# A decoder layer on one core: shared weights split in thirds behind each step's work, up products inside the last four steps, the first SiLUs together, one bank for the last gate's chain

## The chip, the core and the metric

The kernel runs on one core of a Trainium2 chip. The time is that of the device, in microseconds: the median over runs. Profiles are of one execution each.

## What is computed

The reference is one pre-norm decoder layer in float32 on x (8 x 112 x 512), that is 896 tokens:

```
x = x + attention(layernorm(x))          # 16 heads of 128, causal
x = x + cross_attention(layernorm(x), ctx)   # 32 heads of 16, ctx 8 x 375 x 512, q and k rms-normalised
x = x + moe(layernorm(x))
moe(x):
  probs = softmax(x @ gate_w.T); two best of 8 experts, weights normalised
  out = (silu(x @ shared_gate.T) * (x @ shared_up.T)) @ shared_down.T      # inner width 704
  out += sum over the two experts e of w_e * (silu(x @ gate_e.T) * (x @ up_e.T)) @ down_e.T   # inner width 352
```

## The kernel before

Every large product is made of three (`mm3`, L505 to L507): each operand is held as a high part, rounded by ScalarE (`hi`, L953), and a low part, the difference, subtracted by VectorE (L1334) or GpSimd (L1864). Five instruction streams are written out by hand, one function for each engine, and wait for one another on semaphores (`w.wait_ge`). Each engine works in program order, so the order of the calls sets everything.

After the first attention comes the cross attention in NK = 48 steps (batch, half of the heads, a third of the context; `keys`). A step of TensorE (`step` in `tensor`) is: scores of step n (`score_pe`, L702); one thing aside, by turns a transposition of the last unit's output (`out_pe`, L729), a transposition of a normalised batch (`norm_turn`, L593) or a piece of the gate's logits (`gate_pe`); the key and value rows of step n + 4 (`rows_pe`, 12 products of 512 columns from `wkv` and `ctx`), which the last four steps don't have; the transposition of keys (`rows_turn`, L669); values of step n (`value_pe`, L719), which wait for the exponentials of ScalarE (`ee`, L1115). VectorE scales keys (`rq`, `rr`, `kn`), copies them (`kT`) and normalises batches.

The shared expert has six slices of weights (c = 0 to 5, each 128 x 1536 with gate, up and down parts; tiles SE, S1, S2, S0, S1, S2, loaded by SP into `sf_e`, `sf0`, `sf1`). For the first 448 tokens a slice needs: `s_hi_act` and `s_low` (split), `up_pe(0, c, a)` with a = 0 the gate and a = 1 the up product (12 products of 448 columns each), `up_silu`, `up_mul`, `up_hi`, `up_low`, and `down_pe(c, tiles)`, four tiles of three products with 512 columns, added up in banks 2 to 5. I call these up(c,a), silu(c), low(c), down(c). ScalarE has one table for exponential and logarithm and another for silu; a change is an ACT_TABLE_LOAD.

Before, slices 0, 1 and 2 are split ahead of steps 3, 43 and 45, whole on ScalarE, then one third on VectorE and two on GpSimd at the same time. up(0,0), up(0,1), up(1,0), up(1,1) follow the values of steps 44 to 47. The last batch is then normalised, transposed and sent through the gate, and VectorE works out the routing: softmax, two best experts, counts (`t_cum`), a small product on TensorE ("R"), the place of each row (`slot`), the expert of each unit (`eid`). Slices 3, 4, 5 are split and multiplied among this. Normalised rows (`rows_normal`, L1727) go to memory by 16 indirect transfers of GpSimd (`scattered`, L1965), in two groups of eight; SP then loads the gathered units (`xg`, L2116).

The second half is a list of jobs (`job_pe`): the shared expert for the other 448 tokens in three jobs, whose weights are `E` and `F` (`part_hi`, `part_low`), then 21 units of the experts. Its first product is at 787.74 us in the profile, the first transposition of `xg` (L813) at 817.93.

The wait that SP has between the routing and the first gathered unit, and the loads ahead of it, in the kernel's words:

```
                else:
                    w.wait_ge(*scattered[1, NB - 1])
                e.dma_start(xg[j % 4][:, :], slots_d[unit_of[j] * BS:(unit_of[j] + 1) * BS, 2:]).then_inc(*xg_in[j % 4].did(j))

            part_load(0, 0)
            part_load(0, 3)
            sf_load(5)
```

## Time and profile before

| | |
|---|---|
| median of 3 runs | 990.66 us (990.51 to 990.93) |
| the profiled execution | 991.74 us, its span 989.90 us |
| TensorE busy (PE) | 936.6 us, 95% |
| VectorE (DVE) | 553.5 us, 56% |
| ScalarE (ACT) | 452.4 us, 46% |
| GpSimd (POOL) | 192.9 us, 19% |
| chain that ended last | PE 86%, DVE 8%, ACT 2%, all others 1% or less |

A row of the timeline gives start, duration, engine, line, operation, result <- inputs, sizes and count; in brackets the idle time before it and what ended it. Matmuls overlap by their filling and draining, so start to start is the time that one takes up. "PEclk" is the granted clock: 1.00 is 2.4 GHz, 0.50 is 1.2 GHz. `bank` is a bank of PSUM. An index that the names have in the code is left out in the trace.

### The profile page before, as it was taken

Reading aid. Unit: us, or ns where it says so; the run is one execution under the profiler, and the core shown is the slowest. Engines: PE = TensorE matmul, PEld = TensorE weight load, DVE = VectorE, ACT = ScalarE, POOL = GpSimd, SP = SyncE. Lnnn points to the kernel's source line nnn. Section 1 sums busy time; section 2 is a strip of 40 time slices with the busy share of each in tenths; the row PEclk is TensorE's granted clock in tenths of the full one; section 3 lists DMA queues with packets and bytes.
Section 4 is the critical chain, followed back from the end, with each engine's and each line's share of the span. In section 5 each row is a group of like instructions: output and inputs, shape, how many; then the busy total and the mean of one; then the engine's idle time right before and its main releaser. Section 6 shows DMA issues by size and latency. Waiting matters only on the chain.

```text
span 989.9 us, 17898 instructions
## 1 busy us (share of the span) xinstructions
PE 936.6 (95%) x7250; PEld 811.3 (82%) x7250; DVE 553.5 (56%) x1178; ACT 452.4 (46%) x1100; POOL 192.9 (19%) x141
## 2 busy tenths in 40 slices
PE   4999999999999999989999999999788999999995
PEld 3999999999999999866777777777566788899994
DVE  6253535353535353765654654654527655888882
ACT  3342414141414152636665665665543233656651
POOL 1220202020202033302101101101111530222322
PEclk9999999999999999999999999999898999999998
DMA  5110632020202003141100100100112566899973
GB/s 185 66 44 21 223 101 66 22 73 17 76 17 71 2 22 128 43 128 55 33 12 22 33 12 23 32 13 2 65 33 101 202 208 234 276 308 290 294 208 42
DMA packets 31330, 94.12 MB, mean 95 GB/s; under 512 B 6177, under 2 KB 9489, under 8 KB 29329
## 3 DMA queue, kind: packets, MB, share of 16 engines
q1 hardware_dynamic: 26944, 83.80, 24.8%
q0 software_dynamic: 4304, 9.19, 4.7%
q8 instruction: 57, 0.93, 0.4%
q14 instruction: 25, 0.20, 0.1%
HBM read 74.33 MB, written 16.81 MB: 92 GB/s over the span
## 4 chain that ended last, share of the span: by engine, by line
PE 86%; DVE 8%; ACT 2%; issue 1%; DMA 1%; POOL 1%; SPq 0%; ACTq 0%; DVEq 0%
PE bank L505 23%; PE bank L506 22%; PE bank L507 22%; PE bank L702 4%; PE bank L719 4%; PE bank L577 3%; PE bank L552 3%; PE bank L669 2%; DVE E_lo L1334 1%; PE bank L564 1%; DVE rq L1473 1%; PE bank L813 1%; PE bank L729 1%; PE bank L593 1%; PE bank L821 1%
## 5 line engine op out<-in xcount | busy, mean ns | idle before, releaser
L1115 ACT ACTIVATE ee<-bank 125x448 f32<-125x448 f32 x192 | 91.1, 549 | 23.1 <-PE bank L702 22.1
L505 PE MATMUL bank<-xT_hi,wqk_hi 128*128 128x448 f32 x256 | 95.9, 375 | 1.4 <-DVE xT_lo L1334 1.4
L506 PE MATMUL bank<-xT_hi,wqk_lo 128*128 128x448 f32 x256 | 93.6, 366 | 0.0
L507 PE MATMUL bank<-xT_lo,wqk_hi 128*128 128x448 f32 x256 | 93.6, 366 | 0.0
L505 PE MATMUL bank<-wkv_hi,ctx_hi 128*125 128x512 f32 x192 | 81.3, 423 | 8.9 <-DVE kn L1486 8.0
L1334 DVE TENSOR_TENSOR E_lo<-F,E_hi 128x940 fp32r<-128x940 f32 (+2 forms) x62 | 80.8, 1330 | 1.6 <-ACT E_hi L953 1.5
L506 PE MATMUL bank<-wkv_hi,ctx_lo 128*125 128x512 f32 x192 | 77.0, 401 | 0.0
L507 PE MATMUL bank<-wkv_lo,ctx_hi 128*125 128x512 f32 x192 | 76.6, 399 | 0.0
L1864 POOL TENSOR_TENSOR ctx_lo<-ctx_f,ctx_hi 128x500 fp32r<-128x500 f32 x24 | 30.1, 1255 | 216.1 <-ACT ctx_hi L953 216.1
L505 PE MATMUL bank<-wv_hi,xT_hi 128*112 128x256 f32 x256 | 72.2, 282 | 0.0
L506 PE MATMUL bank<-wv_hi,xT_lo 128*112 128x256 f32 x256 | 71.7, 280 | 0.0
L507 PE MATMUL bank<-wv_lo,xT_hi 128*112 128x256 f32 x256 | 71.7, 280 | 0.0
L953 ACT ACTIVATE E_hi<-F 128x940 fp32r<-128x940 f32 (+2 forms) x62 | 67.6, 1147 | 1.1 <-PE bank L507 0.4
L1416 DVE TENSOR_TENSOR xa<-xa,bank 128x512 f32<-128x512 f32 x56 | 38.3, 687 | 53.1 <-PE bank L507 53.1
L1979 POOL DMA_INDIRECT out<-yg,meta x21 | 39.9, 1901 | 141.1 <-DMA out<-yg,meta 70.1
L1864 POOL TENSOR_TENSOR wqk_lo<-wqk_f,wqk_hi 128x1024 fp32r<-128x1024 f32 x16 | 37.8, 2363 | 145.0 <-ACT wqk_hi L953 145.0
L1495 DVE COPY kT<-bank 128x250 f32<-128x250 f32 x48 | 20.1, 418 | 79.8 <-PE bank L669 79.8
L1095 ACT ACTIVATE sq<-bank 125x256 f32<-125x256 f32 (+1 forms) x64 | 24.5, 383 | 83.6 <-PE bank L507 83.6
L953 ACT ACTIVATE qk<-bank 128x448 f32<-128x448 f32 x32 | 17.4, 544 | 97.6 <-PE bank L507 97.6
L1012 ACT ACTIVATE pp<-sm,nm 112x112 f32<-112x112 f32 x128 | 48.1, 377 | 30.3 <-DVE nm L1388 30.3
L505 PE MATMUL bank<-E_hi,xgT_hi 128*128 128x352 f32 x168 | 56.4, 336 | 0.6 <-DVE E_lo L1334 0.6
L507 PE MATMUL bank<-E_lo,xgT_hi 128*128 128x352 f32 x168 | 54.2, 323 | 0.0
(320 smaller groups left out, 2430.7 us busy)
## 6 DMA issues: line engine op xcount, KB each, us to landing
F<-wexp SPq DMA_DIRECT2D x14, 1408.0 KB, 7.5
F<-wexp SPq DMA_DIRECT2D x14, 768.0 KB, 7.3
wqk_f<-wqk SPq DMA_DIRECT2D x16, 512.0 KB, 3.3
ctx_f<-ctx SPq DMA_DIRECT2D x24, 250.0 KB, 2.7
slots<-zt SPq DMA_DIRECT2D x1, 5397.0 KB, 19.1
xg<-slots SPq DMA_DIRECT2D x21, 256.0 KB, 6.5
F<-moe SPq DMA_DIRECT2D x6, 768.0 KB, 6.1
wv_f<-wv SPq DMA_DIRECT2D x8, 512.0 KB, 3.4
```

Source lines behind the costliest of these rows:

```text
L505: e.matmul(out, a[0], b[0], start=first, stop=False)
L506: e.matmul(out, a[1], b[0], start=False, stop=False)
L507: return e.matmul(out, a[0], b[1], start=False, stop=last)
L702: i = e.matmul(SX[r][0:MS, g * 2 * T:(g + 1) * 2 * T], kT[n % 6][32 * r:32 * r + 32, g, :], qT[u % 2][32 * r:32 * r + 32, g, :, :], start= ...
L719: i = e.matmul(AB[32 * c:32 * c + VW, r * T:(r + 1) * T], vb[n % 6][:, 8 * (c // 2) + 2 * r + c % 2, :], ee[(4 * n + r) % 8][:, c * T:(c + ...
L953: return e.activation(out, src, ACT.Copy)
L1012: i = e.activation(pp[g][:, c, :], sm[g][:, c, :], ACT.Exp, bias=nm[g][:, c:c + 1], scale=ISQ, accum_out=rs[g][:, c:c + 1])
L1115: e.activation(ee[(4 * n + r) % 8][:, :], SX[r][0:MS, 0:4 * T], ACT.Exp, scale=0.25).then_inc(*x_exped.did((n, r)))
L1334: return e.tensor_tensor(out, src, high.bitcast(F32), ALU.subtract)
L1416: e.tensor_tensor(xa[:, j, :], xa[:, j, :], PJ[u][:, :], ALU.add).then_inc(*pj_dve.did(u))
L1864: return e.tensor_tensor(out, src, high.bitcast(F32), ALU.subtract)
L1979: e.indirect_dma_start(out_d, bass.IndirectOffsetOnAxis(ap=meta[:, unit_of[j], 0:1].bitcast(U32), axis=0), yg[j % 4][:, :], None, compute_ ...
```

## The change

- Slices are split in thirds of 512 columns (two for the gate and up parts, the last for the down part), on ScalarE and VectorE alone, behind the work of a step: slice 0 in steps 3, 4, 5, slice 1 in step 44, slice 2 in 45, slice 3 in 46. An up product waits for two thirds of its slice, a down product for the third.
- up(0,0) to up(1,1) come before the key transposition and the values of steps 44 to 47. The first gate and up results are copied out of their banks (`gate_keep`, `up_keep`), the silu is applied behind the last step; silu(0), silu(1), silu(2) follow one another there.
- The last gate's chain uses bank 3 alone, so that down products for banks 2, 5 and 4 can stand between; "R" moves behind up(3) to bank 7.
- VectorE's order in the routing is new; rows 0 to 3 are normalised before the expert numbers.
- The two groups of scatters wait for four transfers at a time.

Where lines with "..." stand, parts of the diff are left out.

```diff
-        TX, tx_before, tx_last = {}, {}, {7: ("p", 1), 3: ("s", 1), 4: ("s", 2)}
+        TX, tx_before, tx_last = {}, {}, {7: ("p", 1), 3: ("s", 1)}
         for n, u in enumerate(tx_uses):
-            i = 3 + (n - tx_turn) % 2 if n >= tx_turn else 7
+            i = 3 if n >= tx_turn else 7
             TX[u], tx_before[u], tx_last[i] = banks[i], tx_last[i], u
...
-        ups = [("u", 0, c, a) for c in range(3) for a in range(2)] + ["R"]
-        ups += [("u", 0, c, a) for c in range(3, NS) for a in range(2)]
+        ups = [("u", 0, c, a) for c in range(4) for a in range(2)] + ["R"]
+        ups += [("u", 0, c, a) for c in range(4, NS) for a in range(2)]
...
-        downs = [(0, 0, b) for b in (0, 3, 1, 2)] + [(0, c, b) for c in range(1, NS) for b in range(4)]
+        downs = [(0, c, b) for c, b in ((0, 0), (0, 3), (0, 2), (1, 0), (1, 3), (1, 2), (0, 1), (1, 1), (2, 0), (2, 3), (2, 2), (2, 1))]
+        downs += [(0, c, b) for c in range(3, NS) for b in range(4)]
+        down_end = {c: [d for d in downs if d[1] == c][-1] for c in range(NS)}
...
-        scattered = lane("scattered", [(k, b) for k in range(2) for b in range(NB)])
+        scattered = [[lane(f"scattered{k}{i}", range(4 * i, 4 * i + 4)) for i in range(2)] for k in range(2)]
...
+        s_step = {3: [(0, 0)], 4: [(0, 1)], 5: [(0, 2)], NK - 4: [(1, 0), (1, 1), (1, 2)], NK - 3: [(2, 0), (2, 1), (2, 2)],
+                  NK - 2: [(3, 0), (3, 1), (3, 2)]}
...
                 if n + 4 < NK:
                     rows_pe(*keys[n + 4])
+                else:
+                    up_pe(0, (n - NK + 4) // 2, n % 2)
...
-                if n >= NK - 4:
-                    i = n - NK + 4
-                    up_pe(0, i // 2, i % 2)
...
+            up_pe(0, 2, 0)
             out_pe(NU - 1)
-            up_pe(0, 2, 0)
+            up_pe(0, 2, 1)
+            down_pe(0, (0, 3))
             norm_turn(3, NB - 1)
-            down_pe(0, (0,))
+            down_pe(0, (2,))
+            down_pe(1, (0,))
             gate_pe(NB - 1, 5)
+            down_pe(1, (3,))
             gate_pe(NB - 1, 6)
-            up_pe(0, 2, 1)
-            down_pe(0, (3, 1, 2))
-            down_pe(1)
+            down_pe(1, (2,))
+            down_pe(0, (1,))
+            down_pe(1, (1,))
+            up_pe(0, 3, 0)
+            up_pe(0, 3, 1)
+            down_pe(2, (0, 3))
             w.wait_ge(*oc_done[0])
             w.wait_ge(*tab_in[1])
             w.wait_ge(*cum_done[0])
...
-            down_pe(2)
-            for c in (3, 4, 5):
+            down_pe(2, (2, 1))
+            for c in (4, 5):
                 for a in range(2):
                     up_pe(0, c, a)
-                if c > 3:
-                    down_pe(c - 1)
+                down_pe(c - 1)
...
+                for it in s_step.get(n, []):
+                    s_hi_act(*it)
+                if n == NK - 4:
+                    gate_keep()
+                if m == MC - 1 and n < NK - 1:
                     value_copy(u)
...
-                hi(p[0][:, :], f[:, :]).then_inc(*s_hi.did(c))
+                z = slice(part * 512, part * 512 + 512)
+                hi(p[0][:, z], f[:, z]).then_inc(*s_hi.did((c, part)))
+            def gate_keep():
+                w.wait_ge(*gu_full["u", 0, 0, 0])
+                hi(sg[0][:, :], GU["u", 0, 0, 0][:, 0:HT]).then_inc(*g0_kept.did(0))
...
-                if n == NK - 3:
-                    s_hi_act(2)
                 step(n)
                 if n == 0:
                     w.wait_ge(*gw_in[0])
                     hi(gw[0][:, :, :], gw_f[:, :, :]).then_inc(*gw_hi.did(0))
-                if n == NK - 3:
-                    up_silu(0, 0)
-                    up_hi(0, 0)
-                    exp_table()
+            up_silu(0, 0)
+            value_copy(NU - 1)
+            up_hi(0, 0)
+            up_silu(0, 1)
+            up_silu(0, 2)
+            exp_table()
+            up_hi(0, 1)
             norm_root(3, NB - 1, T)
+            s_hi_act(4, 0)
+            s_hi_act(4, 1)
             w.wait_ge(*tx_full["n", 3, NB - 1])
             norm_hi(3, NB - 1, T, TX["n", 3, NB - 1])
             gate_copy(NB - 1)
             w.wait_ge(*probs_in[0])
             e.activation(small["pr"][:, 0:64], small["pr"][:, 0:64], ACT.Exp).then_inc(*probs_done.did(0))
-            up_silu(0, 1)
-            up_hi(0, 1)
-            up_silu(0, 2)
             up_hi(0, 2)
-            s_hi_act(3)
-            s_hi_act(4)
+            s_hi_act(4, 2)
+            s_hi_act(5, 0)
+            s_hi_act(5, 1)
             up_silu(0, 3)
-            s_hi_act(5)
+            s_hi_act(5, 2)
             up_hi(0, 3)
             part_hi(0, 0)
-            part_hi(0, 3)
             up_silu(0, 4)
...
-            def s_low(c, z):
+            def s_low(c, part):
                 p, f = (ring[c % 3], sf[c % 2]) if c > 1 else ((S1, sf_e) if c else (SE, sf_e))
-                w.wait_ge(*s_hi[c])
-                low(p[1][:, z:], f[:, z:], p[0][:, z:]).then_inc(*s_dve.did(c))
+                w.wait_ge(*s_hi[c, part])
+                z = slice(part * 512, part * 512 + 512)
+                low(p[1][:, z], f[:, z], p[0][:, z]).then_inc(*s_lo.did((c, part)))
+            def up_keep():
+                g = "u", 0, 0, 1
+                w.wait_ge(*gu_full[g])
+                e.tensor_copy(hh[0][:, :], GU[g][:, 0:HT]).then_inc(*u0_kept.did(0))
...
+            up_mul(0, 0)
+            up_low(0, 0)
+            up_mul(0, 1)
             out_scale(NU - 1)
             out_add()
             third_stats(NB - 1)
+            up_low(0, 1)
             norm_out(3, NB - 1)
+            up_mul(0, 2)
             norm_low(3, NB - 1, T, TX["n", 3, NB - 1])
+            s_low(4, 0)
+            s_low(4, 1)
             gate_out(NB - 1)
             def rows_normal(b):
...
+            up_low(0, 2)
+            s_low(4, 2)
+            up_mul(0, 3)
...
-            s_low(4, 0)
+            rows_normal(0)
+            rows_normal(1)
+            up_low(0, 3)
+            s_low(5, 0)
+            s_low(5, 1)
+            rows_normal(2)
+            rows_normal(3)
             le, le2 = (small[i][0:1, :].rearrange("p (j e) -> p j e", e=NE) for i in ("le", "le2"))
...
-            rows_normal(0)
-            rows_normal(1)
-            up_mul(0, 3)
-            up_low(0, 3)
-            rows_normal(2)
-            rows_normal(3)
-            s_low(5, 0)
+            up_mul(0, 4)
             for b in range(4, NB):
                 rows_normal(b)
+            up_low(0, 4)
+            s_low(5, 2)
             part_low(0, 0)
+            up_mul(0, 5)
             part_low(0, 3)
-            up_mul(0, 4)
-            up_low(0, 4)
-            up_mul(0, 5)
             up_low(0, 5)
             for b in range(4):
                 w.wait_ge(*ac_full[0, NS - 1, b])
-            def s_low(c, m):
...
-            s_low(3, SC)
             w.wait_ge(*slot_done[0])
             w.wait_ge(*clear[0])
             w.wait_ge(*numbered[1])
             w.wait_ge(*weighed[0, 1])
             for k in range(2):
-                if k:
-                    w.wait_ge(*scattered[0, NB - 1])
-                    for i in range(2):
+                for i in range(2):
+                    if k:
+                        w.wait_ge(*scattered[0][i][4 * i + 3])
                         e.tensor_copy(rows[i][:, :, 1:2], w01[:, 1, 4 * i:4 * i + 4].unsqueeze(2)).then_inc(*weighed1.did(i))
-                    w.wait_ge(*weighed1[1])
-                for b in range(NB):
-                    w.wait_ge(*rows_n[b])
-                    e.indirect_dma_start(slots_d, bass.IndirectOffsetOnAxis(ap=slot[:, k, b:b + 1], axis=0),
-                                         rows[b // 4][:, b % 4, :], None).then_inc(*scattered.did((k, b)))
+                        w.wait_ge(*weighed1[i])
+                    for b in range(4 * i, 4 * i + 4):
+                        w.wait_ge(*rows_n[b])
+                        e.indirect_dma_start(slots_d, bass.IndirectOffsetOnAxis(ap=slot[:, k, b:b + 1], axis=0),
+                                             rows[i][:, b % 4, :], None).then_inc(*scattered[k][i].did(b))
             def add_back(j):
```

The order of three places, as the program gives it (its line numbers differ by 5 to 40 between the two; `[waits ...]` names the semaphores). TensorE in step 44, before:

```order
L593 MATMUL bank7<-ident_49,xn0_59 128x112 [waits q_copied,xn3]
...
L669 MATMUL bank7<-ident_49,kn1_111 128x125 [waits xT3,kn_done]
...
L719 MATMUL bank6<-ee0_128,vb2_114 32x112 [waits x_exped,squared]
...
L719 MATMUL bank6<-ee3_131,vb2_114 32x112 [waits x_exped]
...
L505 MATMUL bank0<-xT_hi_51,SE_hi_156 128x448 [waits s_pool,s_dve]
L506 MATMUL bank0<-xT_hi_51,SE_lo_157 128x448
L507 MATMUL bank0<-xT_lo_52,SE_hi_156 128x448
...
```

and now, where the first up product of slice 0 (`SE`, bank 0) comes behind the transposition of the normalised batch (`xn0`):

```order
L598 MATMUL bank7<-ident_49,xn0_59 128x112 [waits q_copied,xn3]
...
L510 MATMUL bank0<-xT_hi_51,SE_hi_156 128x448 [waits s_lo]
L511 MATMUL bank0<-xT_hi_51,SE_lo_157 128x448
L512 MATMUL bank0<-xT_lo_52,SE_hi_156 128x448
...
L674 MATMUL bank7<-ident_49,kn1_111 128x125 [waits xT3,kn_done]
...
L724 MATMUL bank6<-ee0_128,vb2_114 32x112 [waits x_exped,squared]
...
```

The up product moved from behind the values (`ee`, `vb2`) to ahead of the keys' transposition (`kn1`); the same holds for steps 45 to 47.

VectorE in the routing, behind the counts (`t_cum`), where the weights of the two experts are worked out (`t_f`, `w`). Before:

```order
L1769 COPY t_cum<-t_sc 112x32 [waits own_dve]
L1770 SCALAR_TENSOR_TENSOR t_f<-t_m_217,t_m_218 112x8
L1771 RECIPROCAL t_f<-t_f 112x8 [waits own_dve]
L1772 TENSOR_TENSOR w_60<-t_m_217,t_f 112x8 [waits own_dve]
L1773 TENSOR_TENSOR w_60<-t_m_218,t_f 112x8 [waits own_dve]
```

Now:

```order
L1799 COPY t_cum<-t_sc 112x32 [waits own_dve]
L1356 TENSOR_TENSOR hs0lo<-sg_166,hs0hi 128x448 [waits h_hi]
L1356 TENSOR_TENSOR S1lo<-sf_159,S1hi 128x512 [waits s_hi]
L1625 TENSOR_TENSOR hh_s<-sg_s,bank 128x448 [waits gu_full,gu_act]
L1803 SCALAR_TENSOR_TENSOR t_f<-t_m_217,t_m_218 112x8
L1804 RECIPROCAL t_f<-t_f 112x8 [waits own_dve]
L1805 TENSOR_TENSOR w_60<-t_m_217,t_f 112x8 [waits own_dve]
L1806 TENSOR_TENSOR w_60<-t_m_218,t_f 112x8 [waits own_dve]
```

Three operations of slices 2, 4 and 3 (`hs0lo`, `S1lo`, `hh_s`) stand in between; `hh_s` waits for its silu.

ScalarE from the exponentials of the routing (`t_pr`) on. Before:

```order
L1309 ACTIVATE t_pr<-t_pr 112x64 [waits probs_in]
L1180 ACT_TABLE_LOAD
L1180 ACTIVATE sg_s<-bank 128x448 [waits gu_full]
L953 ACTIVATE hs_shi<-hh_s 128x448 [waits gu_dve]
L1180 ACTIVATE sg_165<-bank 128x448 [waits gu_full]
L953 ACTIVATE hs0hi<-sg_166 128x448 [waits ac_full,gu_dve]
L953 ACTIVATE S0hi<-sf_160 128x1536 [waits d_sf1]
L953 ACTIVATE S1hi<-sf_159 128x1536 [waits ac_full,d_sf0]
L1180 ACTIVATE sg_s<-bank 128x448 [waits gu_full]
```

Now:

```order
L1333 ACTIVATE t_pr<-t_pr 112x64 [waits probs_in]
L963 ACTIVATE hs0hi<-sg_166 128x448 [waits ac_full,gu_dve]
L963 ACTIVATE S1hi<-sf_159 128x512 [waits ac_full]
L963 ACTIVATE S2hi<-sf_160 128x512 [waits gu_full,d_sf1]
L963 ACTIVATE S2hi<-sf_160 128x512
L1201 ACT_TABLE_LOAD
L1201 ACTIVATE sg_s<-bank 128x448 [waits gu_full]
L963 ACTIVATE S2hi<-sf_160 128x512 [waits ac_full]
L963 ACTIVATE hs_shi<-hh_s 128x448 [waits gu_dve]
```

The silu of slice 3 (`sg_s`) and its table load stood behind the whole casts of slices 3 and 4 (`S0hi`, `S1hi`), and stand now behind two thirds of slice 5 (`S2hi`), which wait for the slice's load (`d_sf1`).

## Rows read from the trace of the kernel before

**Rows 1.** TensorE's windows: length, then busy us (and count) of PE, PEld, DVE, ACT, POOL; PEclk, DMA share, GB/s:

```profile
666.30:669.20 2.90, 2.88 (x12) 2.29 (x13) 2.38 (x9) 1.57 (x5) 0.00 (x0) 1.00 0.35 88
...
705.90:711.20 5.30, 5.30 (x13) 4.00 (x14) 1.73 (x8) 0.00 (x0) 0.00 (x0) 0.50 0.00 0
...
749.00:754.40 5.40, 5.40 (x19) 4.51 (x18) 4.32 (x17) 2.63 (x4) 0.00 (x0) 0.69 0.90 306
...
753.00:754.00 1.00, 1.00 (x6) 0.74 (x5) 0.93 (x4) 0.00 (x0) 0.00 (x0) 1.00 1.02 424
```

**Rows 2.** The timeline of TensorE, steps 37 and 43 to 45, and one row of ScalarE:

```profile
666.32 0.50 PE L505 MATMUL bank<-wkv_hi,ctx_hi 128*125 128x512 f32 x1 [0.59 <-DVE kn L1486]
...
705.90 0.79 PE L505 MATMUL bank<-wkv_hi,ctx_hi 128*125 128x512 f32 x1 [3.60 <-DVE kn L1486]
...
712.82 1.04 PE L702 MATMUL bank<-qT,kT 32*125 32x224 f32 x16
...
716.43 0.97 PE L719 MATMUL bank<-ee,vb 125*32 125x112 f32 x32
...
717.33 0.47 PE L505 MATMUL bank<-xT_hi,SE_hi 128*128 128x448 f32 x1
...
719.96 1.04 PE L702 MATMUL bank<-qT,kT 32*125 32x224 f32 x16
...
721.01 1.85 ACT L1115 ACTIVATE ee<-bank 125x448 f32<-125x448 f32 x4 [1.63 <-PE bank L702]
```

**Rows 3.** The timeline of ScalarE, GpSimd, VectorE and TensorE in steps 3, 43 and 46:

```profile
458.27 0.37 PE L505 MATMUL bank<-wqx,xT_hi 128*112 128x256 f32 x1 [1.58 <-DVE kn L1486]
...
700.54 1.48 ACT L953 ACTIVATE S1hi<-sf_e 128x1536 fp32r<-128x1536 f32 x1
...
702.09 2.85 POOL L1864 TENSOR_TENSOR S1lo<-sf_e,S1hi 128x1024 fp32r<-128x1024 f32 x1 [24.43 <-ACT S1hi L953]
...
702.65 2.32 DVE L1473 SCALAR_TENSOR_TENSOR rq<-rr 125x16 f32<-125x16 f32 x1
...
722.88 1.28 ACT L1180 ACT_TABLE_LOAD   x1
```

**Rows 4.** The timeline of TensorE, the last output's and the last batch's transposition:

```profile
739.36 0.60 PE L729 MATMUL bank<-ident,oo 128*112 128x128 f32 x4
...
743.91 0.60 PE L593 MATMUL bank<-ident,xn 112*128 112x112 f32 x4 [1.51 <-DVE xn L1353]
```

**Rows 5.** The timeline of VectorE, from the last logits through the routing:

```profile
747.81 0.17 DVE L1536 COPY lg<-bank 112x8 f32<-112x8 f32 x1 [2.06 <-PE bank L688]
...
756.81 3.47 DVE L1770 SCALAR_TENSOR_TENSOR t_f<-t_m,t_m 112x8 f32<-112x8 f32 x1
...
765.43 0.17 DVE L1820 CAST slot<-t_vec 112x16 uint32<-112x16 f32 x1
...
769.70 0.98 DVE L1727 TENSOR_SCALAR rows<-xs,mv,rstd 112x512 f32<-112x512 f32 x2
...
776.81 3.43 DVE L1334 TENSOR_TENSOR E_lo<-F,E_hi 128x1536 fp32r<-128x1536 f32 x2
```

**Rows 6.** The timeline of SP, loads of F and of the first gathered units:

```profile
748.89 0.90 SPq L2101 DMA_DIRECT2D F<-moe  x2
...
811.17 1.76 SPq L2116 DMA_DIRECT2D xg<-slots  x4
```

**Rows 7.** The timeline of GpSimd, the first, the fourth and the last scatter:

```profile
771.17 1.12 POOL L1965 DMA_INDIRECT slots<-rows,slot  x1 [10.91 <-DVE rows L1727]
...
776.41 4.64 POOL L1965 DMA_INDIRECT slots<-rows,slot  x1 [0.30 <-issue]
...
801.37 0.94 POOL L1965 DMA_INDIRECT slots<-rows,slot  x1 [0.30 <-issue]
```

**Rows 8.** The timeline of TensorE, the second half's first product and first gathered unit:

```profile
787.74 0.37 PE L505 MATMUL bank<-xT_hi,E_hi 128*128 128x448 f32 x1
...
817.93 0.60 PE L813 MATMUL bank<-ident,xg 128*128 128x128 f32 x4
```

More of the change, by code:

```diff
@@ L449, in decoder_layer @@
         gl_done, lg_done = sig("gl_done", range(NB)), sig("lg_done", range(NB))
-        NC0 = range(NS)
-        s_hi = sig("s_hi", NC0)
-        s_dve = sig("s_dve", [c for c in NC0 if c != 3])
-        s_pool = sig("s_pool", range(4))
+        third = [(c, p) for c in range(NS) for p in range(3)]
+        s_hi, s_lo = sig("s_hi", third), sig("s_lo", third)
+        g0_kept, u0_kept = sig("g0_kept", [0]), sig("u0_kept", [0])
         gu_full = sig("gu_full", ups)
@@ L1182, in up_silu @@
             def up_silu(n, c):
+                if n == 0 and c == 0:
+                    w.wait_ge(*g0_kept[0])
+                    e.activation(sg[0][:, :], sg[0][:, :], ACT.Silu).then_inc(*gu_act.did(("u", 0, 0)))
+                    return
                 if n == 0 and c > 1:
@@ L1592, in up_mul @@
                 w.wait_ge(*gu_full[g])
+                if n == 0 and c == 0:
+                    w.wait_ge(*u0_kept[0])
+                    e.tensor_tensor(h_[1][:, :], h_[0][:, :], h_[1][:, :], ALU.mult).then_inc(*gu_dve.did(("u", n, c)))
+                    return
                 e.tensor_tensor(h_[1][:, :], h_[0][:, :], GU[g][:, 0:HT], ALU.mult).then_inc(*gu_dve.did(("u", n, c)))
@@ L1705, in vector @@
             for n in range(NK):
-                if n == 3:
-                    s_low(0, 1024)
-                if n == NK - 5:
-                    s_low(1, 1024)
+                step(n)
+                for it in s_step.get(n, []):
+                    s_low(*it)
                 if n == NK - 3:
-                    s_low(2, 1024)
-                step(n)
-                if n == NK - 3:
-                    up_mul(0, 0)
-                    up_low(0, 0)
+                    up_keep()
+            up_mul(0, 0)
+            up_low(0, 0)
+            up_mul(0, 1)
             out_scale(NU - 1)
@@ L1757, in vector @@
             e.tensor_tensor(oc, oh[0], oh[1], ALU.add).then_inc(*oc_done.did(0))
-            up_low(0, 2)
             w.wait_ge(*oc_done[0])
@@ L2066, in sf_load @@
                 k = c - 2 if c > 3 else 0 if c == 1 else None
-                if k is not None and k != 3:
-                    w.wait_ge(*s_dve[k])
-                if k is not None and k < 4:
-                    w.wait_ge(*s_pool[k])
+                if k is not None:
+                    w.wait_ge(*s_lo[k, 2])
                 e.dma_start((sf_e if c < 2 else sf[c % 2])[:, :], moe_d[c]).then_inc(*sf_in[c % 2].did(c))
@@ L2114, in xg_load @@
                 else:
-                    w.wait_ge(*scattered[1, NB - 1])
+                    for i in range(2):
+                        w.wait_ge(*scattered[1][i][4 * i + 3])
                 e.dma_start(xg[j % 4][:, :], slots_d[unit_of[j] * BS:(unit_of[j] + 1) * BS, 2:]).then_inc(*xg_in[j % 4].did(j))
```

43 lines of the change are left out of this document (13 added, 30 removed).

## The prediction, written before the changed kernel ran

> **What bounds the kernel now.** The page first: TensorE is busy nearly all the span, in the chain that ended last too, so only a stretch where it idles or runs slowly can give time back. The slices show two, near 705 and 745 us. I read the windows there, TensorE's timeline against them, then the engine that each gap names. From 787.74 [rows 8] nothing is reordered, and a shift of that moment should reach the end whole unless a transfer comes late.
>
> TensorE idles 3.60 us before 705.90, where the same product in step 37 waited 0.59 [rows 2]; the 12 products then take 5.30 us at a granted clock of 0.5 (the 1.2 GHz level), 2.90 at 1.0 [rows 1]. The idle has its origin on VectorE: a 125x16 operation lasts 2.32 us, from 702.65, because GpSimd's `S1lo` runs from 702.09 for 2.85 us; before it ScalarE casts all of slice one for 1.48 us [rows 3]. Step 3 shows it too: TensorE waits 1.58 us at 458.27 [rows 3]. And `t_f`, 112x8, takes 3.47 us in the routing arithmetic [rows 5]. I measure from TensorE's score product of step 44, 712.82 [rows 2], called t = 0.
>
> **Sum, part one: up to step 44.** The cast and the subtraction go behind the step's work, GpSimd's share is gone. Idle falls from 3.60 to 0.65, the block from 5.30 to 2.90 us [rows 1]: 5.35 saved. In step 3, 1.58 goes; its thirds in steps 3 to 5 fall between other vector work, where a transposition or a key can be late by 0.3 twice: 1.0 saved (ends: 0 and 1.85). Casting 1536 columns takes 1.48 us [rows 3], so a third is 0.5; subtracting twice as many takes VectorE 3.43 (`E_lo`, 776.81) [rows 5], so a third is 0.6. The splitting costs some 0.1 us per slice and engine by this, of which two slices lie on VectorE's path. The Trainium skill speaks against it: "VectorE: DVE Perf Modes", section on the TRN2 errata, says that operations read from SBUF pay a fixed latency each, a large tile once and many small ones each time. By its 224 fixed cycles on ScalarE 12 extra casts would be an estimated 2.2 us, mostly off the path; no row here separates it.
>
> **Part two: steps 44 to 47 to the last logits.** Before, each up product stands behind the values, and TensorE waits for exponentials first. Per step I take 0.97 for scores (1.04 with the end that overlaps, 719.96), 2.63 for an up product (717.33 to 719.96), 0.90 for values (716.43 to 717.33) [rows 2]; transpositions and the gate products between add 2.2 over four steps (estimate). 4 x 4.50 + 2.2 = 20.2 us, against 712.82 to 739.36 [rows 2, 4] = 26.54. The exponentials start 1.05 us after the score (721.01 against 719.96) and take 1.85 [rows 2]; they now have 3.6 before the values, so no wait. What has to be ready: slices one to three are cast behind the exponentials (1.5 each), subtracted by t = 6.8, 10.6 and 15.9; up(1,0) on TensorE at 12.1 and up(1,1) at 16.7 need the two copies, made at 5.3 and 10.6. Both copies (0.5) are hidden so. The late one next is the silu: the table load of 1.28 us [rows 3] now stands before `value_copy` of the last unit, which ends at 20.8; TensorE reads it only at 22.8, behind up(2,0). From that transposition to the last normalisation's, the chain of VectorE took 4.55 (739.36 to 743.91) [rows 4]; it is kept: t = 27.4. up(2,1) and two down tiles fill TensorE meanwhile, so the slow clock of the next products (0.5, where before it stood idle in this chain) should not come. From 743.91 to the logits' copy at 747.81 [rows 4, 5] were 3.90; with the gate products at 2.4 GHz but down(1,3) ahead of the last transposition, 3.6. **Logits at t = 31.05**, before 34.99: 3.94 saved.
>
> **Part three: logits to slots.** 747.81 to 765.60 [rows 5] = 17.8 us. Up to `t_cum` it took 9.0; without the four operations of products one and two that stood among it, an estimated 5.8 (0.6 each, and two waits for ScalarE of 0.4): t = 36.85. Then up_low(0,2) and a third of slice four: 38.0. **up_mul(0,3) now stands ahead of the weights, and waits for its silu, which stands behind two casts of slice five.** That slice is the third of three loads of 768 KB. Two issued from 748.89 [rows 6] filled 749 to 754.4 at 306 GB/s [rows 1]; a third at the last full microsecond's 424 GB/s adds 1.9, so it lands 8.5 after the logits: 39.55. Casts 1.0, table 1.28, silu 0.55, product 0.6: 43.0. The rest took 5.3 from 760.28 (756.81 + 3.47) to 765.60 [rows 5]; with its first operation 5.5. **Slots at 48.5**, 17.45 after the logits: 0.35 saved. So GpSimd's 3.47 us stall is nearly replaced by a wait of 4.4 for slice five. Behind that wait stand all VectorE work, down(3) on TensorE and the scatters.
>
> **Part four: slots to the second half.** 765.60 to 787.74 [rows 5, 8] = 22.1. VectorE now, in order: two rows 0.95, low(3) 0.55, two thirds 1.2, two rows 0.95, the expert numbers 2.5 (765.60 to 769.70 less the 1.7 of `S1lo` that stood there), product 0.55, four rows 1.9, low(4) 0.6, a third 0.6, `E_lo` 1.7, product 0.5, `E_lo` 1.7, low(5) 0.6 [rows 5] = 14.3: t = 62.8. Then down(5), 12 products of 512 columns like the block of part one, 2.85, and 0.1: **65.75**, 17.25 after slots, 4.9 saved. TensorE's own list from gate6 at 30.9 is 29.55 us, to 60.45, so VectorE ends it; TensorE idles 3.4 before down(3) (46.6 to 50.0) and 2.1 before down(5).
>
> **Sum.** 1.0 + 5.35 + 3.94 + 0.35 + 4.9 = 15.5 us. The profiled execution took 991.74 (span 989.90), so 976.2; the median of the three runs stands 1.08 below it, hence **975.2 us**. A measurement can tell 0.2%, 2 us, from no change.
>
> **Does a transfer come late?** The scatters were issued from 771.17 to 801.37, and SP was let go at 811.17 [rows 6, 7], 8.9 after the last one's end. The first now goes at t = 50, which is 756.5 in the profile's time: 14.7 earlier. A pause of nearly 5 us between the two groups, for landing, goes too, since group two now waits for four transfers that are long done: an estimated 25.5 from first to last instead of 30.2, so the last goes at 75.5 and SP at 85.3. TensorE needs the first gathered unit 30.2 after the half's start (817.93) [rows 8], at 95.9. That leaves 10.6 us for its load; before there were 6.8, and it was enough.
>
> **Rivals.**
> A. The wait for slice five isn't there (loads are shared out otherwise, or land by t = 35). Then up_mul(0,3) runs at 38.0 and 4.4 more goes: TensorE's 60.45 nearly binds. 970.8. For it: only the order of issue says that the slice lands last. Against it: the three loads are 2.36 MB, and 5.4 us at 306 GB/s moved 1.65 [rows 1].
> B. The clock falls in the new idle before down(3). An idle of 3.60 was followed by 5.3 us at 0.5 [rows 1, 2], and 3.4 is near it. down(3) then takes 2.4 more, hidden by VectorE; but the gap at 60.7 can repeat it at the second half's start: +2.4, and the last silu +0.9: 977.6 to 978.5. Waits in steps 44 to 47 that I don't see have this size also.
> C. The scatters come late by a little. GpSimd's issue from 776.41 took 4.64 us, beside `E_lo` on VectorE; others 0.94 [rows 7]. If fifteen can only go from t = 62.8 on, 1.24 apart, the last ends at 81.4, SP goes at 90.3 and the unit is there by 97.1: +1.2, and with the experts' loads in the way up to +10: 976.4 to 985.
> D. **Slower.** The same mechanism on all: VectorE is now busy without a pause behind the slots and later with `E_lo`. At 4.94 us each the sixteenth ends at t = 125, SP goes at 133.9, the unit is there at 140.7: 44.8 late, 1020 us. It decides from a mean spacing of 3.0 us, where the gain of 15.5 is used up; before it was 2.0 (30.2 over 15). "SBUF — State Buffer" of the Trainium skill (The "DVE blocks DMA" trap) has GpSimd locked out of writing descriptors while VectorE holds the shared port in a two-port mode, which would speak for D with the rows' tensor-scalar operations; the 4.64 beside a tensor-tensor is longer than that rule explains.
> E. The gain stays away: TensorE's order is new, but each up product in front only moves the wait to the values, and the chain of the last batch is as long as before. Against it stand the 3.6 us that the exponentials get. 990.
>
> **Chances.** Forecast 0.66, A 0.09, B 0.15, C 0.05, D 0.03, E 0.02. Faster 0.95, same 0.02, slower 0.03. The range takes the forecast's bounds (step 3: +1.0 and -0.85; slice five: -4.4; clock: +3.3; C's small end +1.2): 970.5 to 981.5; about 0.1 lies outside.
>
> **What the profile after would show.** The wkv block of step 43 at clock 1.0 after an idle under 1 us; the score of step 44 near 706.5; no GpSimd subtraction after `ctx_lo`; steps 44 to 47 in 20 us with no wait before values; the logits near 737.5. On VectorE an idle of 4 us before `hh_s`, released by ScalarE, whose cast of `S2hi` waited for a DMA; slots near 755; TensorE idle 3 us at `hs_slo` before down(3); the second half from 772.2; SP's wait for scatters under 8 us short of TensorE's use. Wrong it would be if steps 44 to 47 took over 23 us, if the clock fell there, or if TensorE waited for `xg`.

## The result, and the profile after

The changed kernel takes 976.65 us (median of 4 runs, 975.54 to 977.98), the kernel before 990.59 (4 runs, 990.39 to 990.93): ratio 0.986, 95% interval 0.9842 to 0.9877. It is faster by 1.4%, 1.45 us above the forecast of 975.2 and inside its range. The profiled execution took 977.98 us, its span 976.2; the one of before took 991.74, span 989.90. The kernel before isn't equally fast in every set of runs: in the two sets of the experiments below its medians were 992.91 and 992.99 us, so against those a kernel as fast as the changed one gains some 16.3 us instead of 13.9. The forecast of 15.5 lies between.

The window of TensorE that answers to 705.90:711.20 of [rows 1], and those between the moments that the forecast names (length, then busy us and count of PE, PEld, DVE, ACT, POOL; PEclk, DMA share, GB/s):

```profile
701.80:704.90 3.10, 3.06 (x14) 2.43 (x14) 1.87 (x8) 1.66 (x5) 0.00 (x0) 1.00 0.00 0
706.30:725.85 19.55, 19.55 (x265) 16.09 (x264) 9.93 (x21) 15.24 (x32) 0.00 (x0) 1.00 0.32 120
725.85:736.60 10.75, 10.62 (x65) 8.49 (x62) 7.73 (x18) 6.49 (x13) 0.00 (x0) 1.00 0.01 2
736.60:755.70 19.10, 15.44 (x75) 12.94 (x75) 11.38 (x58) 7.35 (x11) 0.73 (x17) 1.00 0.35 131
755.70:773.80 18.10, 16.39 (x61) 12.82 (x62) 15.81 (x31) 3.08 (x4) 14.00 (x11) 0.81 0.62 201
...
757.20:762.40 5.20, 5.20 (x12) 3.80 (x13) 4.93 (x16) 0.05 (x1) 4.29 (x4) 0.50 0.30 92
```

The block of step 43 runs at full clock; steps 44 to 47 (second line) hold no idle time at all. TensorE loses time behind the logits, in two ways. It idles for 3.66 us before the slots (19.10 less 15.44) and 1.71 behind them (18.10 less 16.39); 4.80 of it is one gap before down(3), which lies across the border of the two windows. And the clock behind the slots is 0.81 on average, which the last line places: the 12 products of down(3) ran at 0.50.

The timeline of TensorE after, which answers to [rows 2], [rows 4] and [rows 8]:

```profile
701.84 0.50 PE L510 MATMUL bank<-wkv_hi,ctx_hi 128*125 128x512 f32 x1 [0.64 <-DVE kn L1508]
...
706.30 1.04 PE L707 MATMUL bank<-qT,kT 32*125 32x224 f32 x16
...
728.39 0.60 PE L734 MATMUL bank<-ident,oo 128*112 128x128 f32 x4
...
732.93 0.60 PE L598 MATMUL bank<-ident,xn 112*128 112x112 f32 x4
...
757.19 0.77 PE L510 MATMUL bank<-S0hi,hs_shi 128*112 128x512 f32 x1 [4.80 <-DVE hs_slo L1356]
...
770.90 0.48 PE L510 MATMUL bank<-S2hi,hs_shi 128*112 128x512 f32 x1 [0.21 <-DVE hs_slo L1356]
...
773.78 0.37 PE L510 MATMUL bank<-xT_hi,E_hi 128*128 128x448 f32 x1
```

The score of step 44, t = 0 of the forecast, is at 706.30 instead of 712.82, the second half starts at 773.78 instead of 787.74 [rows 8]. That is 13.96 us, and the span is 13.7 shorter: all but 0.3 of what is won by the second half's start reaches the end.

VectorE and ScalarE from the last logits to the slots and beyond, which answer to [rows 5]:

```profile
736.55 0.17 DVE L1558 COPY lg<-bank 112x8 f32<-112x8 f32 x1 [0.57 <-PE bank L693]
...
749.68 0.62 DVE L1625 TENSOR_TENSOR hh_s<-sg_s,bank 128x448 f32<-128x448 f32 x1 [6.09 <-ACT sg_s L1201]
...
755.52 0.17 DVE L1853 CAST slot<-t_vec 112x16 uint32<-112x16 f32 x1
...
765.33 1.75 DVE L1356 TENSOR_TENSOR E_lo<-F,E_hi 128x1536 fp32r<-128x1536 f32 x1
768.01 0.62 DVE L1625 TENSOR_TENSOR hh_s<-sg_s,bank 128x448 f32<-128x448 f32 x1 [0.94 <-PE bank L512]
...
746.64 1.15 ACT L963 ACTIVATE S2hi<-sf 128x512 fp32r<-128x512 f32 x2 [7.21 <-DMA sf<-moe]
747.81 1.28 ACT L1201 ACT_TABLE_LOAD   x1
```

The wait that the forecast put behind the third load is there, and it is longer: VectorE stands still for 6.09 us, because ScalarE waited 7.21 for slice five before its casts, its table and the silu of slice three. The lines of SP and GpSimd that answer to [rows 6] and [rows 7]:

```profile
737.63 0.90 SPq L2119 DMA_DIRECT2D F<-moe  x2
738.58 0.43 SPq L2090 DMA_DIRECT2D sf<-moe  x1
...
787.02 2.19 SPq L2135 DMA_DIRECT2D xg<-slots  x4
...
757.08 2.29 POOL L1986 DMA_INDIRECT slots<-rows,slot  x1 [19.49 <-DVE rows L1761]
...
764.93 2.95 POOL L1986 DMA_INDIRECT slots<-rows,slot  x1 [0.30 <-issue]
...
782.01 2.18 POOL L1986 DMA_INDIRECT slots<-rows,slot  x1 [0.30 <-issue]
```

The gathered units are asked for at 787.02, and TensorE's first transposition of one is at 803.93 with no wait before it. No gathered unit came late; slice five is the one load that was waited for.

### The profile page after: what moved, and what is told of

It is laid out like the page before. It is cut to its first block, busy times and chain, and to the rows that moved or that the text cites. A ratio compares the mean times of both kernels' runs of the same rounds, so it can differ in the third digit from the quotient of the medians.

```text
span 976.2 us, 17918 instructions
## 1 busy us (share of the span) xinstructions
PE 932.0 (95%) x7250; PEld 809.7 (83%) x7250; DVE 552.7 (57%) x1192; ACT 454.3 (47%) x1113; POOL 179.9 (18%) x137
## 4 chain that ended last, share of the span: by engine, by line
PE 88%; DVE 6%; DMA 2%; ACT 2%; issue 1%; POOL 1%; SPq 1%; DVEq 0%; ACTq 0%
PE bank L510 24%; PE bank L511 23%; PE bank L512 23%; PE bank L707 4%; PE bank L724 4%; PE bank L582 3%; PE bank L557 3%; PE bank L674 2%; PE bank L569 1%; PE bank L734 1%; DVE E_lo L1356 1%; PE bank L820 1%; DMA sf<-moe 1%; PE bank L598 1%; PE bank L828 1%
```

## The experiments

In both sets of runs the kernel before scattered more than any other (989.92 to 995.97), and the changed kernel itself was in neither. So each edit of the changed kernel is compared by its median with the kernel of its own set that is nearest to the changed one: 976.73 (scatters in two steps) in the first, 976.61 (slices whole) in the second. Both agree with the changed kernel's 976.65.

**The load of slice five ahead.** Nothing else is touched.

```diff
-            for c in range(2, 5):
+            for c in range(2, 6):
                 sf_load(c)
...
             part_load(0, 3)
-            sf_load(5)
```

> The changed kernel, with the load of slice five issued right behind that of slice four instead of behind the routing table and F. Theory 1 (VectorE's routing waits 6.1 us for a silu that stands behind slice five's late load, and VectorE then ends the stretch): the product hh_s follows at once, slots come 5 to 6 us earlier against the logits (13.5 instead of 19.1 us), TensorE's idle before down(3) shrinks from 4.8 to under 1 us with no fall of the clock, and the kernel takes 971.5 to 973.5 us, ratio to the kernel before about 0.982. TensorE's own list of products then binds, so not all 6 us come through. Theory 2 (the wait is covered by other work and TensorE's list binds already): the wait goes but the time stays at 976 to 977.

Measured: 971.23 us (970.76 to 972.02), ratio 0.9782 (0.9763 to 0.9802). VectorE, ScalarE and TensorE in it:

```profile
743.00 0.62 DVE L1625 TENSOR_TENSOR hh_s<-sg_s,bank 128x448 f32<-128x448 f32 x1 [0.24 <-PE bank L512]
...
749.00 0.17 DVE L1853 CAST slot<-t_vec 112x16 uint32<-112x16 f32 x1
...
739.68 1.28 ACT L1201 ACT_TABLE_LOAD   x1
...
763.34 0.49 PE L510 MATMUL bank<-S2hi,hs_shi 128*112 128x512 f32 x1 [1.84 <-DVE hs_slo L1356]
```

The wait for ScalarE is gone, the slots come 13.45 us after the logits (735.72 to 749.17) instead of 19.14, and down(3) has no idle before it. Of these 5.7 us 5.5 reach the end. So the place of slice five's load, third behind two others, is what put the wait there. down(5) now waits 1.84, and is the next thing late.

**The product of slice three behind the slots.** The load stays where the change put it; the product that waits for it no longer stands ahead of the routing.

```diff
             s_low(4, 2)
-            up_mul(0, 3)
...
+            up_mul(0, 3)
             rows_normal(0)
             rows_normal(1)
             up_low(0, 3)
```

> The changed kernel, with VectorE's product of slice three moved behind the slots, loads unchanged. Theory 1: the slots come 6 us earlier (13 us after the logits), the scatters too, but low(3) for TensorE's down(3) still cannot be before the silu of slice three at about 13 us after the logits, so it comes 4 to 5 us earlier than in the changed kernel; time 972 to 974.5. Theory 2 (what counts is only when TensorE's products are fed by slice five's chain, not the routing): 976 to 977, with the wait moved to just behind the slots.

Measured: 973.07 us (971.85 to 973.54), ratio 0.9804 (0.9781 to 0.9827), 3.7 below the set's comparison. VectorE:

```profile
749.96 0.17 DVE L1852 CAST slot<-t_vec 112x16 uint32<-112x16 f32 x1
750.04 0.61 DVE L1625 TENSOR_TENSOR hh_s<-sg_s,bank 128x448 f32<-128x448 f32 x1
```

The silu of slice three is as late as before, but no routing stands behind it. Both runs say the same of the mechanism from two sides: a load and one position in VectorE's list, and changing either removes the wait ahead of the routing. The late load isn't free even so: by the medians this kernel is 1.8 us behind the first experiment's. The two profiles, 971.85 and 972.02 us, are as fast as each other and don't show where that is lost.

**The up products back behind the values** of steps 44 to 47, all else as changed.

```diff
                     rows_pe(*keys[n + 4])
-                else:
-                    up_pe(0, (n - NK + 4) // 2, n % 2)
...
                 step(n)
+                if n >= NK - 4:
+                    up_pe(0, (n - NK + 4) // 2, n % 2)
```

> The changed kernel, with up(0,0) to up(1,1) put back behind the values of steps 44 to 47. If the 6.1 us between the score of step 44 and the last output's transposition (26.5 before, 22.1 now with one more up product in it) come from the place of these products: the four steps take 24.5 to 26 us again instead of 19.6, time 980.5 to 983. Rival: the steps got shorter because the silu table loads and GpSimd's share left them, and the place of the products is worth under 2 us: 977 to 979.

Measured: 982.36 us (981.88 to 983.12), ratio 0.9894 (0.9871 to 0.9918), 5.6 above the set's comparison. TensorE's timeline:

```profile
706.12 1.04 PE L707 MATMUL bank<-qT,kT 32*125 32x224 f32 x16
...
709.40 0.65 PE L674 MATMUL bank<-ident,kn 125*128 125x125 f32 x2 [1.70 <-DVE xT_lo L1356]
709.98 1.72 PE L724 MATMUL bank<-ee,vb 125*32 125x112 f32 x32
...
728.43 1.62 PE L724 MATMUL bank<-ee,vb 125*32 125x112 f32 x32 [0.70 <-ACT ee L1125]
...
734.94 0.60 PE L734 MATMUL bank<-ident,oo 128*112 128x128 f32 x4
```

The window of TensorE there (columns as above):

```profile
709.40:712.70 3.30, 3.30 (x37) 2.56 (x38) 2.22 (x4) 1.61 (x4) 0.00 (x0) 0.50 0.18 68
```

And a line of TensorE in the kernel before, the values of step 46:

```profile
729.28 1.71 PE L719 MATMUL bank<-ee,vb 125*32 125x112 f32 x32 [1.65 <-ACT ee L1115]
```

From the score of step 44 to the last output's transposition it takes 28.82 us, against 22.09 in the changed kernel; without up(2,0), which stands ahead of the transposition in both (2.43), that is 26.39, against 26.54 before [rows 2, 4]. The waits for the key's turn and for exponentials are back. 6.7 us are lost there and 5.6 at the end.

That 26.39 and 26.54 are so near is chance; two differences cancel. Behind the 1.70 of idle the clock fell here and not before: the key's transposition takes 0.58 instead of 0.34, and from the values of step 44 to the next score it takes 4.78 us, before 3.53 (716.43 to 719.96) [rows 2], 1.5 in all. In step 46, on the other hand, the kernel before waited for exponentials that stood behind a load of the exponential's table: score to values took it 3.41 us (725.87 to 729.28), here 1.74 (720.68 to 722.42). These loads have left the steps with the change, and stay out of them in this experiment. So of the 6.9 us that the whole change took off the four steps (26.54 to 19.66 without up(2,0)), some 5.2 are the place of the up products and 1.7 the table loads. The rival, which gave the place under 2 us, is refuted; the table loads that it named are real, but the smaller part.

**The second group of scatters waits for all of the first**, as before the change.

```diff
-                        w.wait_ge(*scattered[0][i][4 * i + 3])
+                        w.wait_ge(*scattered[0][0][3])
+                        w.wait_ge(*scattered[0][1][7])
```

> The changed kernel, with GpSimd's second group of scatters again waiting for all eight of the first. If the first gathered unit is in time with room: TensorE sees no wait for it, the last scatter goes 3 to 4 us later, time unchanged at 975.5 to 978. Rival (with the second half 14 us earlier, the units are just in time): TensorE waits 1 to 4 us at its first gathered unit, 978 to 981.

Measured: 976.73 us (975.99 to 977.32), ratio 0.9841 (0.9818 to 0.9864): the changed kernel's time. GpSimd waits 6.06 us in it (`777.16`, released by the scatter's landing). Its last scatter goes 6.9 us later, counted from the logits, and not 3 to 4; SP asks for the first gathered unit at 796.41, 5.7 us before TensorE uses it (802.11) instead of 16.9, and TensorE still sees no wait. This part of the change is covered and worth nothing here.

**Slice one by VectorE alone, in the kernel before**, at the old place.

```diff
                 if n == NK - 5:
-                    s_low(1, 1024)
+                    s_low(1, 0)
```

(and GpSimd's share of slice one is taken out)

> The kernel before with one edit: slice one, ahead of step 43, is subtracted by VectorE alone (1536 columns, about 1.7 us), GpSimd has no share. Theory 1 (GpSimd's subtraction holds up VectorE's small operation; the origin of the 3.60 us idle): the 125x16 operation falls from 2.3 us to under 0.2; VectorE's path is then 1.7 in place of a third of 0.6 and a stall of 2.3, so TensorE's idle before the block of step 43 is about 2.4 instead of 3.60; 1.2 us faster than before if the clock still falls to half (ratio 0.9988), 3.6 if the idle of 2.4 leaves it at full (0.9964). Theory 2 (ScalarE's whole cast and the subtraction's length make the idle, GpSimd's part is harmless): the idle grows by 1.1 to 4.7 us, ratio 1.001.

Measured: 990.65 us (12 runs, 988.55 to 993.08), ratio 0.9977 (0.9963 to 0.999). The timeline of VectorE and TensorE:

```profile
703.23 1.76 DVE L1334 TENSOR_TENSOR S1lo<-sf_e,S1hi 128x1536 fp32r<-128x1536 f32 x1 [0.50 <-ACT S1hi L953]
704.91 0.17 DVE L1473 SCALAR_TENSOR_TENSOR rq<-rr 125x16 f32<-125x16 f32 x1
...
706.01 0.50 PE L505 MATMUL bank<-wkv_hi,ctx_hi 128*125 128x512 f32 x1 [2.51 <-DVE kn L1486]
```

The windows of that block and of up(0,0) in step 44 (columns as above):

```profile
706.01:710.46 4.45, 4.45 (x13) 3.42 (x14) 1.73 (x8) 0.20 (x1) 0.00 (x0) 0.62 0.00 0
...
716.50:720.70 4.20, 4.20 (x16) 3.48 (x12) 0.69 (x1) 1.92 (x2) 2.05 (x1) 0.59 0.00 0
```

Theory 1 holds: the 125x16 operation takes 0.17 us where it took 2.32 [rows 3], so GpSimd's subtraction was what held it. 2.15 us of stall go and 1.1 of longer subtraction come, and the idle is 2.51 instead of 3.60 [rows 2]: what is left is put down to the slice's own work, which stands ahead of the key; the next experiment moves it. The clock still fell, later in the block, and once more in step 44, so the gain lies between the two values expected. That holds for the profile; of the twelve runs six took 988.55 to 989.85 us at a mean granted clock of 0.993, and six 991.44 to 993.08 at 0.988 to 0.991.

**Slice one behind step 44, in the kernel before**: whole on ScalarE, shared by VectorE and GpSimd, only the place is new.

```diff
-                if n == NK - 5:
-                    s_hi_act(1)
...
                 step(n)
+                if n == NK - 4:
+                    s_hi_act(1)
```

(`s_low(1, 1024)` of VectorE and GpSimd in the same way)

> The kernel before with one edit: slice one is cast and subtracted behind step 44 instead of ahead of step 43, whole on ScalarE and shared by VectorE and GpSimd as it was. Theory 1 (the place was the fault, not the size of the pieces): the idle before step 43's block falls below 1 us, its 12 products run at full clock in 3.1 us, 4 to 5.3 us saved, ratio 0.9947 to 0.9960. Theory 2 (only thirds on two engines fit in there): the cast and the stalled VectorE hold up the exponentials or the keys of steps 44 and 45, TensorE idles there instead, 3 us or more are given back, ratio 0.998 or above.

Measured: 988.47 us (985.34 to 989.28), ratio 0.9958 (0.9945 to 0.9971). The timeline of TensorE, GpSimd and VectorE:

```profile
702.86 0.50 PE L505 MATMUL bank<-wkv_hi,ctx_hi 128*125 128x512 f32 x1 [0.64 <-DVE kn L1486]
...
713.96 2.87 POOL L1864 TENSOR_TENSOR S1lo<-sf_e,S1hi 128x1024 fp32r<-128x1024 f32 x1 [36.38 <-ACT S1hi L953]
...
715.28 2.10 DVE L1334 TENSOR_TENSOR S2lo<-sf,S2hi 128x512 fp32r<-128x512 f32 x1 [0.68 <-ACT S2hi L953]
```

The window of TensorE there (columns as above):

```profile
702.86:705.76 2.90, 2.90 (x13) 2.29 (x14) 1.83 (x8) 1.61 (x5) 0.00 (x0) 1.00 0.00 0
```

The idle is 0.64 and the block 2.90 at full clock. Measured from the key wait of step 3 (457.95, which this kernel still has) to the score of step 44 (707.31) it takes 249.36 us, against 254.55 before (458.27 [rows 3] to 712.82 [rows 2]): 5.19 won by the place alone (4.5 by the medians of the set, 992.99 and 988.47). The last output's transposition comes 26.56 us after the score of step 44, before it was 26.54. Nothing is given back, though GpSimd's subtraction still stalls VectorE there (2.10 us for 512 columns): no key is due in those steps. So the gain before step 43 needed neither thirds nor GpSimd's absence, only the place. Step 3 was not tried by itself.

**Slices one to three whole, in the changed kernel**, at the same places.

```diff
+                if c in (1, 2, 3):
+                    if part == 0:
...
+                        hi(p[0][:, :], f[:, :]).then_inc(s_hi.sem, 3)
+                    return
                 z = slice(part * 512, part * 512 + 512)
                 hi(p[0][:, z], f[:, z]).then_inc(*s_hi.did((c, part)))
```

(`s_low` in the same way)

> The changed kernel with one edit: slices one, two and three are cast and subtracted whole (1536 columns), by the same engines and at the same places. Theory 1 (a third costs a third, 0.1 us or less more for the splitting; nothing waits for it in steps 44 to 47): time within 0.5 us of the changed kernel, ratio 0.985 to 0.987; the whole cast lasts 1.48 us and the whole subtraction 1.74, against three times 0.53 and three times 0.6 from start to start. Theory 2 (a fixed latency for each operation that reads SBUF, as the Trainium skill says in VectorE: DVE Perf Modes, is paid by each third): 12 operations fewer take up to 2 us off the two engines, and 1 to 2 us off the steps, ratio 0.984 or below.

Measured: 976.61 us (976.02 to 976.9), ratio 0.9837 (0.9823 to 0.9851). The timeline of VectorE and ScalarE in this kernel:

```profile
710.46 1.76 DVE L1362 TENSOR_TENSOR S1lo<-sf_e,S1hi 128x1536 fp32r<-128x1536 f32 x1
...
708.84 1.51 ACT L963 ACTIVATE S1hi<-sf_e 128x1536 fp32r<-128x1536 f32 x1
```

and in the changed one:

```profile
710.93 1.88 DVE L1356 TENSOR_TENSOR S1lo<-sf_e,S1hi 128x512 fp32r<-128x512 f32 x3
...
709.49 1.70 ACT L963 ACTIVATE S1hi<-sf_e 128x512 fp32r<-128x512 f32 x3
```

A slice in thirds costs 0.12 us more on VectorE and 0.19 on ScalarE, 0.06 and 0.1 for each added operation. From the score of step 44 (705.65) to up(2,0) (725.20) both kernels take 19.55, and the times are the same. The rule of the Trainium skill that was weighed (VectorE: DVE Perf Modes, TRN2 errata) holds in direction: several small operations do cost more than one. Its size is too small to matter in this kernel, and the thirds of slices one to three bring nothing either, since no product waits for a whole slice here. Slices zero, four and five stayed in thirds; their cutting was not tried.

**The load ahead, and slice five's product before the subtractions** of 1536 columns: the version that the first experiment points to.

```diff
-            part_low(0, 0)
             up_mul(0, 5)
-            part_low(0, 3)
+            part_low(0, 0)
             up_low(0, 5)
+            part_low(0, 3)
```

(with the first experiment's edit)

> The changed kernel with two edits: the load of slice five ahead, as in the first experiment (971.2 us), and on VectorE the product and the low part of slice five each ahead of one subtraction of 1536 columns (E_lo). Theory 1 (with the load early, down(5) waits 1.84 us for hs_slo, since both E_lo stand ahead of the product's low part): that wait goes, down(5) starts at about 761.7 instead of 763.34, and 1.6 us are saved, 3 if its products also run at full clock then: 968 to 969.6 us, ratio 0.975 to 0.977. Theory 2 (TensorE is held by the second E_lo's weights, or the transfers behind it, a little later): the gap moves to the second half's start and the time stays at 971.

Measured: 969.25 us (968.75 to 969.97), ratio 0.9765 (0.975 to 0.9779). The timeline of TensorE:

```profile
761.50 0.49 PE L510 MATMUL bank<-S2hi,hs_shi 128*112 128x512 f32 x1 [0.23 <-DVE hs_slo L1356]
...
764.37 0.37 PE L510 MATMUL bank<-xT_hi,E_hi 128*128 128x448 f32 x1
```

The window of TensorE from the logits to the second half (columns as above):

```profile
735.60:764.40 28.80, 28.57 (x136) 24.02 (x137) 26.73 (x88) 10.27 (x15) 12.41 (x26) 1.00 0.46 149
```

down(5) starts at 761.50 instead of 763.34, at full clock; TensorE is idle for 0.23 us in this whole stretch. 7.4 us below the set's comparison, it beats both kernels; from here on the order of waits has nothing more to give between the logits and the second half.

## Why the prediction was right

The chain of the forecast held, and its errors cancelled in part: two parts gave 0.17 and 0.80 us more than said, two gave 1.70 and 0.85 less, one of these with the wrong sign. That the time came out within 1.5 us is partly luck. By its parts, in the two profiled executions:

| | forecast | measured |
|---|---|---|
| part one, up to the score of step 44 | 6.35 | 6.52 (712.82 to 706.30) |
| part two, to the logits | 3.94 | 4.74 (34.99 less 30.25) |
| part three, logits to slots | 0.35 | -1.35 (17.79 before, 19.14 after): lost, not won |
| part four, slots to the second half | 4.9 | 4.05 (22.14 before, 18.09 after) |
| sum | 15.5 | 13.96 |

**Part one: right, and its cause right in the main.** 5.35 was said for step 43, the place alone gave 5.19. GpSimd's subtraction did hold VectorE (2.32 us with it, 0.17 without), but that was no more than 1.1 of the 3.60 of idle; cast and subtraction ahead of the key made the rest, up to the 0.64 that is left. In step 3 the wait fell from 1.58 and a later 0.64 to one of 0.85 in the changed kernel: 1.4 where 1.0 was said.

**Part two: right, mis-sized by 0.8.** No value waited, as said. Steps 44 to 47 took 19.55 and not 20.2: the 2.2 us for transpositions and gate products between the blocks were too many. The chain of the last batch kept its length, 4.54 (728.39 to 732.93), and the clock stayed at 1.00. By the third experiment 1.7 us of this part come from the table loads that left the steps, which the forecast did not set apart.

**Part three: the mechanism right, the load's term too small, and so a loss instead of a gain.** "A third at the last full microsecond's 424 GB/s adds 1.9, so it lands 8.5 after the logits": slice five was cast 10.1 us after them (736.55 to 746.64). The stretch moved 307 GB/s on average, while the 424 came from one full microsecond of two loads:

```profile
738.00:746.00 8.00, 8.00 (x43) 7.08 (x42) 5.01 (x22) 1.21 (x2) 0.00 (x0) 1.00 0.81 307
```

2.36 MB at 307 GB/s are 7.7 us, and the start and end of the transfers came on top: 9.0 from the first issue. The mean over a whole transfer, 306 GB/s in [rows 1], had been nearer. The steps behind it were right: 3.66 to the end of the product (3.45 said), 5.39 from there to the slots (5.5 said). The 3.47 us of the operation `t_f` [rows 5] are gone, it takes 0.16 at 750.22, and VectorE had its work ahead of the wait done 7.0 us after the logits, as said (6.95). Rival A, that the wait isn't there, was wrong for this kernel, and the first experiment made its condition true by hand: 971.2 against its 970.8, a gain of 5.5 where it had said 4.4.

**Part four: one term off, and rival B's clock in it.** TensorE idled 4.80 us before down(3), not 3.4: it had run out of work at t = 46.1 (46.6 said), and the low part came 0.9 later with the load; down(3) then ran at 0.50 and took 5.26. VectorE's list covered most of that: of 2.4 us only 0.94 came through, as VectorE's wait for the bank of up(5,1) at 768.01. The forecast had said that this is hidden, and then 2.1 of idle before down(5); it was 0.21. Rival B's condition, a fall of the clock in down(3), came true; its second fall, at the second half's start, which would have made it slower than the forecast, did not.

**Transfers: right, with more room than said.** The sixteen issues took 24.9 us from first to last (25.5 said), and SP was let go 16.9 us before the unit was used (10.6 said). Rivals C and D did not happen, though single scatters were lengthened.

Rival E, that the wait only moves to the values, is refuted by the changed kernel's own steps: 19.55 us without idle time. The third experiment shows that the place of the up products does most of it.

## What to carry to other kernels

An operation on an engine that works in order costs what stands behind it: slice five's load cost the routing nothing until a product whose silu stood behind it came ahead of the routing, and moving either one gave 3.7 to 5.5 us. Where a piece of work is early enough, its place in the order was worth microseconds here, and the cutting of slices one to three into pieces nothing. When loads share the queues, take the mean rate of a whole transfer for the last one's landing, not its best microsecond.
